# A vision tower on one core: the convolution's bias and the first layernorm's rows from one short line

## The chip, the cores and the metric

The kernel runs on one core of one Trainium2 chip. Times are device microseconds of that core. TensorE is called PE in the profile (PEld is its weight loads), VectorE is DVE, ScalarE is ACT, GpSimd is POOL, SyncE is SP. Before the change the median of three runs is 130.71 us (130.52 to 131.06).

## What is computed

Two images of 32 x 128 x 128 go through a patch embedding, a transformer of two layers with linear attention, one more linear attention and a mixed feed-forward layer. The change touches only the start of it:

```
patches = im.reshape(b, c, hp, P, wp, P)                     # 8 x 8 patches, 256 per image
x = einsum('bchpwq,dcpq->bhwd', patches, conv_w)             # contraction over 2048
x = x.reshape(b, hp * wp, -1) + conv_b                       # 256 tokens x 128
for i in range(2):
    y = _ln(x, ln1_g[i], ln1_b[i])                           # (x - mean) * rsqrt(var + eps) * g + b
    qkv = y @ qkv_w[i]
    ...                                                      # softmax of q and k, context, output, feed-forward
```

## The kernel before

The program of each engine is written out by hand, and each engine runs it in order; semaphores tie them together. Tokens lie on the 128 partitions, in two tiles for each image. SyncE issues all loads on one queue (L262 is the helper), in the order of L273 to L296: five pieces of embed_sb, which holds the convolution's weights and the first image's patches, with the bias tile convb_sb after the third; then the first half of the second image's patches, the broadcast load of norm_rows_sb[0] (gain and offset of the first layernorm, one row of 256 numbers written to all partitions), the key weights, small_sb (the identity for transposes, and columns), the query weights, and the rest.

TensorE multiplies in fp32; one product shows as two MATMUL records. It starts with products of ones (L311, warm_up), then adds the 16 chunks of image 0 into two banks (L320), each chunk as soon as its piece of embed_sb is there, and closes each bank with a bias product (L325): all ones, 128 x 128, times convb_sb, whose first row is the bias and whose other rows are zero. It goes on with chunks 0 to 5 of image 1, waits for the normalised y of image 0, turns it (L329), does chunks 6 and 7, and then the keys and queries of image 0 (L341, L347 for queries, L353, L360 for keys), each split in a high and a low part. L360 reads yT_lo, which VectorE makes. Chunks 8 to 15 and the bias of image 1 are worked in between; before the last bias product stand mix_fc_masks (L425 and L427, over nine rows). Then k and q of image 0 are turned (L366, L371), the keys of y are formed (L376) and y of image 1 is turned (L329 again).

The first layernorm of image 0 goes over four engines. VectorE takes the moments out of the bank (L929) and their aggregate (L935), ScalarE copies x out of it (L1514), VectorE centres and multiplies by the gain (L939), GpSimd raises the variance to the power of -0.5 for both tiles at once (L1782), VectorE scales and adds the offset (L944). ScalarE rounds the key and query weights and the turned y to their high parts (L1514), VectorE makes their low parts (L962).

The lines of VectorE around the load are:

```
dve.wait_ge(conv_done, 2)
moments(0, 1, CONV_BANK[0][1][:, 0:D]).then_inc(moments_done, 1)
dve.wait_ge(mean1_ready, 1)
dve.wait_ge(x_ready, 1)
dve.wait_ge(loaded["rg"], 16)
centre_and_gain(0, 0).then_inc(centred1, 1)
dve.wait_ge(moments_done, 2)
mean_and_variance(0, 1, stats).then_inc(mean1_ready, 1)
```

Of the kernel before, what the change touches and what calls it, by code (L numbers as in the profile page):

```python
# [12 lines left out]
P = 128  # L13
# [3 lines left out]
TILES = TOKENS // P  # L17
D = 128
KCONV = CHANNELS * PATCH * PATCH // P
# [34 lines left out]
CONV_AT = (0, 1, 4, 8, 12, KCONV)  # L54
CONV_PIECES = len(CONV_AT) - 1


def build(nc, small, convb, norm_rows0, norm_rows1, embed0, patches1, qkv_w, rest_w, rows, mix, fc_w, proj_w,
          head_w, aqkv_w, aout_w, out):
    with ExitStack() as ctx:  # L60
        def sb(name, shape, dt=F32):
            return ctx.enter_context(nc.sbuf_tensor(name, shape, dt))

        def sem(name):
            return ctx.enter_context(nc.semaphore(name))
# [14 lines left out]

        convb_sb = sb("convb_sb", [P, D])
        norm_rows_sb = [sb(f"norm_rows_sb{l}", [P, GROW]) for l in range(LAYERS)]
# [41 lines left out]
        def bias_row(name, n=0, width=D):  # L124
# [24 lines left out]
        kexp = sb("kexp", [P, PAIRS, TOKENS])  # L149
        ktok = sb("ktok", [P, TILES, INNER])  # L150
        q = sb("q", [P, TILES, INNER])
        qn = sb("qn", [P, TILES, INNER])
# [28 lines left out]
        bank = [ctx.enter_context(nc.psum_tensor(f"bank{i}", [P, 512], F32)) for i in range(8)]  # L181

        HROW_BANK = bank[6]
        CONV_BANK = [(bank[1], bank[5]), (bank[3], bank[6])]
# [29 lines left out]
        loaded = {n: sem(f"loaded_{n}") for n in (  # L214
            "aout", "aqkv", "cb", "embed0", "embed1", "embed2", "embed3", "embed4", "fc", "head",
            "mix", "patches1a", "patches1b", "proj", "qkv0k", "qkv0q", "qkv1", "rest0", "rest1",
            "rg", "rows", "small", "v0")}
        aqkv_weight_high, attention3_columns, attention3_ready, attention3_turned, attention_done, centred1 = (
# [33 lines left out]
        y_ready, y_turned = (  # L252
            sem(n) for n in ("y_ready", "y_turned",))
        consts_set = sem("consts_set")
        stored = sem("stored")
# [4 lines left out]
        def _(sp):  # L260
            def load(dst, src, name):
                sp.dma_start(dst, src).then_inc(loaded[name], 16)  # L262
# [12 lines left out]
            load_embed(4, 8, "embed2")  # L275
            load(convb_sb[:], convb, "cb")
            load_embed(8, 12, "embed3")
            load_embed(12, 16, "embed4")
            load_patches(0, 8, "patches1a")
            load(norm_rows_sb[0][:], norm_rows0.to_broadcast([P, GROW]), "rg")  # L280
            load(qkvw[0][:, INNER:2 * INNER], qkv_w[0][:, INNER:2 * INNER], "qkv0k")
# [25 lines left out]
        def _(pe):  # L307
# [15 lines left out]

            def conv_bias(i, t):
                return nc.tensor.matmul(CONV_BANK[i][t][:, 0:D], ones[:, 0:P], convb_sb[:], start=False, stop=True)  # L325

# [194 lines left out]
            conv(0, 6, 7)  # L521
            conv(0, 7, 8)
            pe.wait_ge(loaded["embed3"], 16)
            conv(0, 8, 9)
# [6 lines left out]
            conv(0, 14, 15)  # L531
            conv(0, 15, 16)
            pe.wait_ge(loaded["cb"], 16)
            conv_bias(0, 0).then_inc(conv_done, 1)
            conv_bias(0, 1).then_inc(conv_done, 1)
            pe.wait_ge(loaded["patches1a"], 16)
            conv(1, 0, 2)
            conv(1, 2, 4)
            conv(1, 4, 6)
# [25 lines left out]
            conv(1, 12, 14)  # L565
            conv(1, 14, 16)
            conv_bias(1, 0).then_inc(conv_done, 1)
            pe.wait_ge(k_exp_ready, 4)
            turn_k(0, 0, 1).then_inc(k_turned, 1)
            pe.wait_ge(coefficients_ready, 1)  # L570
            mix_fc_masks()
            conv_bias(1, 1).then_inc(conv_done, 1)
            pe.wait_ge(q_shifted, 2)
# [353 lines left out]
        def _(dve):  # L927
            def moments(i, t, src):
                return nc.vector.bn_stats(stats[i][:, t, 0:6], src)  # L929
# [4 lines left out]
            def mean_and_variance(i, t, of):  # L934
                return nc.vector.bn_aggr(mv[i][:, t, :], of[i][:, t, :])  # L935
# [159 lines left out]
            dve.wait_ge(conv_done, 2)  # L1095
            moments(0, 1, CONV_BANK[0][1][:, 0:D]).then_inc(moments_done, 1)
            dve.wait_ge(mean1_ready, 1)
            dve.wait_ge(x_ready, 1)
            dve.wait_ge(loaded["rg"], 16)
            centre_and_gain(0, 0).then_inc(centred1, 1)  # L1100
            dve.wait_ge(moments_done, 2)
            mean_and_variance(0, 1, stats).then_inc(mean1_ready, 1)
            dve.wait_ge(mean1_ready, 2)
            dve.wait_ge(x_ready, 2)
            centre_and_gain(0, 1).then_inc(centred1, 1)
            dve.wait_ge(deviation1_ready, 1)
            scale_and_offset(0, 0).then_inc(y_ready, 1)
            dve.wait_ge(centred1, 2)
# [403 lines left out]
        def _(act):  # L1512
            def evict(dst, src):
                return nc.scalar.activation(dst, src, ACT.Copy)  # L1514
# [49 lines left out]
            def gelu3(i, c):  # L1564
                src = FC3_BANK[i][c // 2][:, (c % 2) * TOKENS:(c % 2 + 1) * TOKENS]
                return nc.scalar.activation(hid3[i][:, c, :], src, ACT.Gelu_apprx_tanh, bias=fcb[:, c:c + 1])  # L1566

            act.wait_ge(moments_done, 1)
            evict(x[0][:, 0, :], CONV_BANK[0][0][:, 0:D]).then_inc(x_ready, 1)
# [403 lines left out]
```

## Time and profile before

| | |
|---|---|
| median of three runs | 130.71 us |
| the profiled execution | 130.16 us, of which 128.4 us are span |
| TensorE busy | 117.3 us, 91% of the span |
| VectorE, ScalarE, GpSimd busy | 75.5, 63.8, 48.7 us |
| chain that ended last | TensorE 60%, VectorE 14%, DMA 9% |
| data moved | 12.18 MB, nearly all in the first 33 us |

The span runs from the first to the last instruction of one execution; the median of the runs is 0.55 us above the profiled one. A row of a timeline gives the start, the time from there to the end of a merged group, the engine, the line and the operation, and in brackets how long the engine was idle before it and what it waited for. Records of pipelined products overlap, so the pace of TensorE is read from the starts, not from the durations.

### The profile page before, as it was taken

The numbers are of one execution on the slowest core, as the hardware profiler recorded it, in microseconds if no ns is written. First come the engines' busy times: TensorE is split into PE (matmuls) and PEld (weight loads), VectorE is DVE, ScalarE is ACT, GpSimd is POOL, SyncE is SP. The second block draws the span as 40 slices with busy tenths as digits, with TensorE's granted clock in tenths as the row PEclk, the third lists the DMA queues.
The fourth block names the chain that finished last, engine by engine and source line by source line (L and its number), as shares of the span: only waits on it lengthen the run. The fifth ranks groups of instructions, "written<-read, shape, count | busy, mean of one in ns | idle before, by whom it ended". The sixth has DMA issues, their size and how long they took to land.

```text
span 128.4 us, 2242 instructions
## 1 busy us (share of the span) xinstructions
PE 117.3 (91%) x852; PEld 101.4 (79%) x852; DVE 75.5 (59%) x236; ACT 63.8 (50%) x151; POOL 48.7 (38%) x60
## 2 busy tenths in 40 slices
PE   6999969999999999998999798769889988999991
PEld 6999968986976798996856687757588777998990
DVE  5000384988678963779999866348588477155002
ACT  3000153745578586477774459633872835423520
POOL 0000024043896584416759546096309022032000
PEclk9999999999999999999999999999999999999999
DMA  4999899999100000000000000000000000000101
GB/s 106 373 428 416 242 434 370 406 421 398 50 0 0 0 3 5 0 0 0 0 0 5 0 0 3 0 5 3 0 0 0 0 0 5 0 0 0 61 0 61
DMA packets 3884, 12.18 MB, mean 95 GB/s; under 512 B 441, under 2 KB 1817, under 8 KB 3618
## 3 DMA queue, kind: packets, MB, share of 16 engines
q1 hardware_dynamic: 3874, 12.05, 24.8%
q8 instruction: 6, 0.10, 0.3%
q14 instruction: 4, 0.03, 0.1%
HBM read 11.65 MB, written 0.39 MB: 94 GB/s over the span
## 4 chain that ended last, share of the span: by engine, by line
PE 60%; DVE 14%; DMA 9%; ACT 7%; POOL 4%; issue 3%; SPq 3%; DVEq 0%; POOLq 0%
DMA norm_rows_sb<-in_norm_rows 9%; PE bank L505 6%; PE bank L376 4%; PE bank L419 4%; PE bank L400 4%; PE bank L320 3%; SPq L262 3%; PE bank L341 3%; PE bank L371 3%; PE bank L393 2%; PE bank L353 2%; PE bank L491 2%; PE bank L329 2%; PE bank L407 2%; POOL rstd L1782 2%
## 5 line engine op out<-in xcount | busy, mean ns | idle before, releaser
L1782 POOL TENSOR_TENSOR rstd<-mv,minus_half 128x2 f32<-128x2 f32 x14 | 10.0, 714 | 39.4 <-DVE mv L935 39.1
L1800 POOL TENSOR_TENSOR qn<-q,rqsum 128x512 f32<-128x512 f32 x8 | 8.3, 1044 | 12.3 <-DVE rqsum L995 12.3
L1566 ACT ACTIVATE patches_sb<-bank,fcb 128x256 f32<-128x256 f32 x12 | 5.1, 471 | 10.5 <-PE bank L502 10.5
L1524 ACT ACTIVATE kexp<-bank,nkmax 128x256 f32<-128x256 f32 x16 | 7.5, 472 | 5.7 <-DVE nkmax L975 5.7
L419 PE MATMUL bank<-restw,hid 128*128 128x128 f32 x64 | 8.8, 281 | 1.0 <-ACT hid L1540 1.0
L505 PE MATMUL bank<-projw,patches_sb 128*128 128x192 f32 x48 | 9.4, 331 | 0.0
L400 PEld LDWEIGHTS bank<-cw,qT 128*128 128x128 f32 x64 | 7.8, 192 | 1.6 <-issue 1.0
L419 PEld LDWEIGHTS bank<-restw,hid 128*128 128x128 f32 x64 | 7.8, 191 | 1.6 <-ACT hid L1540 1.4
L400 PE MATMUL bank<-cw,qT 128*128 128x128 f32 x64 | 8.4, 277 | 0.4 <-DVE x L1010 0.4
L320 PEld LDWEIGHTS bank<-embed_sb 128*128 128x128 f32 x64 | 8.1, 203 | 0.1
L320 PE MATMUL bank<-embed_sb 128*128 128x128 f32 x64 | 8.2, 285 | 0.0
L1540 ACT ACTIVATE hid<-bank,small_sb 128x256 f32<-128x256 f32 x16 | 6.5, 473 | 3.2 <-PE bank L414 3.2
L505 PEld LDWEIGHTS bank<-projw,patches_sb 128*128 128x128 f32 x48 | 7.6, 189 | 0.5 <-ACT patches_sb L1566 0.4
L376 PE MATMUL bank<-ktok,y 128*128 128x512 f32 x16 | 8.0, 612 | 0.0
L1514 ACT ACTIVATE x<-bank 128x128 f32<-128x128 f32 x4 | 1.1, 282 | 13.8 <-DVE stats L929 13.8
L1536 ACT ACTIVATE cw<-bank,rksum 128x128 f32<-128x128 f32 x16 | 4.8, 366 | 6.4 <-PE bank L393 5.3
L320 PE MATMUL bank<-embed_sb,patches_sb 128*128 128x128 f32 x64 | 7.9, 277 | 0.0
L929 DVE BATCH_NORM_STATS2 stats<-bank 128x6 f32<-128x128 f32 x4 | 1.1, 275 | 11.0 <-PE bank L325 11.0
L320 PEld LDWEIGHTS bank<-embed_sb,patches_sb 128*128 128x128 f32 x64 | 7.5, 192 | 0.1
L975 DVE TENSOR_REDUCE nkmax<-bank 128x2 f32<-128x512 f32 x8 | 5.4, 688 | 3.0 <-PE bank L360 2.9
L1792 POOL TENSOR_TENSOR xb<-x,rows_sb 128x256 f32<-128x256 f32 x8 | 5.9, 737 | 1.9 <-DVE y L944 1.2
L311 PE MATMUL bank<-ones 128*128 128x192 f32 x16 | 5.2, 487 | 1.1 <-DVE stats L1083 1.1
(167 smaller groups left out, 335.5 us busy)
## 6 DMA issues: line engine op xcount, KB each, us to landing
embed_sb<-in_embed SPq DMA_DIRECT2D x3, 768.0 KB, 6.9
patches_sb<-in_patches SPq DMA_DIRECT2D x2, 1024.0 KB, 11.9
restw<-in_rest_w SPq DMA_DIRECT2D x2, 768.0 KB, 16.5
qkvw<-in_qkv_w SPq DMA_DIRECT2D x3, 256.0 KB, 11.1
qkvw<-in_qkv_w SPq DMA_DIRECT2D x1, 768.0 KB, 16.6
fcw<-in_fc_w SPq DMA_DIRECT2D x1, 768.0 KB, 19.1
embed_sb<-in_embed SPq DMA_DIRECT2D x1, 576.0 KB, 4.3
aqkvw<-in_aqkv_w SPq DMA_DIRECT2D x1, 576.0 KB, 11.8
```

The lines of the kernel that those rows point to most:

```text
L311: mm = nc.tensor.matmul(dst[:, 0:E], ones[:, 0:P], ones[:], start=True, stop=True)
L320: mm = nc.tensor.matmul(CONV_BANK[i][t][:, 0:D], left, embed_sb[:, c, 0:D], start=(c == 0), stop=False)
L376: return nc.tensor.matmul(YK_BANK[s][:], y[s % IMAGES][:, t, :], ktok[:, t, :], start=(t == 0), stop=(t == TILES - 1))
L400: mm = nc.tensor.matmul(ATT_BANK[s][t][:, 0:D], qT[:, t, c * P:(c + 1) * P], cw[:, c, :], start=(c == 0), stop=(c == PAIRS - 1))
L419: mm = nc.tensor.matmul(FF2_BANK[s][t][:, 0:D], hid[:, c, t * P:(t + 1) * P], ff2w(s // IMAGES, c), start=(c == 0), stop=(c == FC - 1))
L505: return nc.tensor.matmul(PROJ3_BANK[i][t][:, 0:E], hid3[i][:, c, t * P:(t + 1) * P], projw[:, c, :], start=(c == 0), stop=(c == HC - 1))
L975: return nc.vector.tensor_reduce(nkmax[i][:, 2 * b:2 * b + 2], K_BANK[s][b][:].rearrange("p (c t) -> p c t", c=2), AX_X, ALU.max, negate=True)
L1524: return nc.scalar.activation(kexp[:, c, :], K_BANK[s][c // 2][:, (c % 2) * TOKENS:(c % 2 + 1) * TOKENS], ACT.Exp, bias=nkmax[i][:, c:c + ...
L1540: return nc.scalar.activation(hid[:, c, :], FF1_BANK[s][c // 2][:, (c % 2) * TOKENS:(c % 2 + 1) * TOKENS], ACT.Gelu, bias=col("ff1_b", s / ...
L1782: return nc.gpsimd.tensor_tensor(rstd[i][:], mv[i][:, :, 1], minus_half[:], ALU.pow)
L1792: return nc.gpsimd.tensor_tensor(xb[i][:], x[i][:], row.unsqueeze(1).to_broadcast([P, TILES, D]), ALU.add)
L1800: return nc.gpsimd.tensor_tensor(qn[:, t, :].rearrange("p (h d) -> p h d", h=HEADS), q[:, t, :].rearrange("p (h d) -> p h d", h=HEADS), rq ...
```

## The change

The bias tile and the broadcast load go. One line of 384 numbers (bias, gain, offset) is loaded on one partition, in a corner of ktok, which isn't written before. Products over one row (ones[0:1] times the line) spread it: the bias straight into the convolution's banks, in the middle of the accumulation, for image 0 after chunk 7 and for image 1 after its chunk 1; gain and offset into a free bank, from which ScalarE copies them to norm_rows_sb[0] before its first other work. The last chunk closes each bank now. In VectorE's program the aggregate of the second tile moves ahead of the first centring, the wait for the load becomes one for the copied rows, and the first scaling waits for the first centring.

```diff
@@ build
-        convb_sb = sb("convb_sb", [P, D])
+        first_row_sb = ktok[0:1, 0, 0:D + GROW]
+        FIRST_ROWS_BANK = bank[2]
@@ SyncE
-            load(convb_sb[:], convb, "cb")
+            load(first_row_sb, first_row, "first_row")
             load_embed(8, 12, "embed3")
             load_embed(12, 16, "embed4")
             load_patches(0, 8, "patches1a")
-            load(norm_rows_sb[0][:], norm_rows0.to_broadcast([P, GROW]), "rg")
@@ TensorE
-            def conv_bias(i, t):
-                return nc.tensor.matmul(CONV_BANK[i][t][:, 0:D], ones[:, 0:P], convb_sb[:], start=False, stop=True)
+            def conv_last(i, t):
+                c = KCONV - 1
+                left = (embed_sb[:, c, D + t * P:D + (t + 1) * P] if i == 0
+                        else patches1_sb[:, c, t * P:(t + 1) * P])
+                return nc.tensor.matmul(CONV_BANK[i][t][:, 0:D], left, embed_sb[:, c, 0:D], start=False, stop=True)
+
+            def conv_bias(i):
+                for t in range(TILES):
+                    mm = nc.tensor.matmul(CONV_BANK[i][t][:, 0:D], ones[0:1, 0:P], first_row_sb[:, 0:D],
+                                          start=False, stop=False)
+                return mm
+
+            def first_norm_rows():
+                return nc.tensor.matmul(FIRST_ROWS_BANK[:, 0:GROW], ones[0:1, 0:P], first_row_sb[:, D:D + GROW],
+                                        start=True, stop=True)
             conv(0, 7, 8)
+            pe.wait_ge(loaded["first_row"], 16)
+            conv_bias(0)
+            first_norm_rows().then_inc(first_rows_done, 1)
             pe.wait_ge(loaded["embed3"], 16)
...
-            conv(0, 15, 16)
-            pe.wait_ge(loaded["cb"], 16)
-            conv_bias(0, 0).then_inc(conv_done, 1)
-            conv_bias(0, 1).then_inc(conv_done, 1)
+            conv_last(0, 0).then_inc(conv_done, 1)
+            conv_last(0, 1).then_inc(conv_done, 1)
             pe.wait_ge(loaded["patches1a"], 16)
             conv(1, 0, 2)
+            conv_bias(1)
             conv(1, 2, 4)
...
-            conv(1, 14, 16)
-            conv_bias(1, 0).then_inc(conv_done, 1)
+            conv(1, 14, 15)
+            conv_last(1, 0).then_inc(conv_done, 1)
             pe.wait_ge(k_exp_ready, 4)
             turn_k(0, 0, 1).then_inc(k_turned, 1)
             pe.wait_ge(coefficients_ready, 1)
             mix_fc_masks()
-            conv_bias(1, 1).then_inc(conv_done, 1)
+            conv_last(1, 1).then_inc(conv_done, 1)
@@ VectorE
             moments(0, 1, CONV_BANK[0][1][:, 0:D]).then_inc(moments_done, 1)
+            dve.wait_ge(moments_done, 2)
+            mean_and_variance(0, 1, stats).then_inc(mean1_ready, 1)
             dve.wait_ge(mean1_ready, 1)
             dve.wait_ge(x_ready, 1)
-            dve.wait_ge(loaded["rg"], 16)
+            dve.wait_ge(first_rows_ready, 1)
             centre_and_gain(0, 0).then_inc(centred1, 1)
-            dve.wait_ge(moments_done, 2)
-            mean_and_variance(0, 1, stats).then_inc(mean1_ready, 1)
             dve.wait_ge(mean1_ready, 2)
             dve.wait_ge(x_ready, 2)
             centre_and_gain(0, 1).then_inc(centred1, 1)
             dve.wait_ge(deviation1_ready, 1)
+            dve.wait_ge(centred1, 1)
             scale_and_offset(0, 0).then_inc(y_ready, 1)
@@ ScalarE
+            act.wait_ge(first_rows_done, 1)
+            evict(norm_rows_sb[0][:], FIRST_ROWS_BANK[:, 0:GROW]).then_inc(first_rows_ready, 1)
             act.wait_ge(moments_done, 1)
```

## Rows read from the trace of the kernel before

**Rows 1.** The page, busy time: us, share of the span, instructions.
```profile
PE 117.3 (91%) x852; PEld 101.4 (79%) x852; DVE 75.5 (59%) x236; ACT 63.8 (50%) x151; POOL 48.7 (38%) x60
```

**Rows 2.** The chain that ended last, in order of time: start, us, what.
```profile
4.39 11.18 DMA norm_rows_sb<-in_norm_rows
```

**Rows 3.** Timeline of TensorE's products, 8 to 20 us.
```profile
8.03 5.52 PE L320 MATMUL bank<-embed_sb 128*128 128x128 f32 x48
13.39 0.61 PE L325 MATMUL bank<-convb_sb,ones 128*128 128x128 f32 x4
13.88 2.94 PE L320 MATMUL bank<-embed_sb,patches_sb 128*128 128x128 f32 x24
17.82 0.44 PE L329 MATMUL bank<-small_sb,y 128*128 128x128 f32 x2 [0.99 <-DVE y L944]
18.09 1.06 PE L320 MATMUL bank<-embed_sb,patches_sb 128*128 128x128 f32 x8
...
19.11 0.28 PE L353 MATMUL bank<-yT_hi,qkw_lo 128*128 128x256 f32 x1
19.36 0.39 PE L360 MATMUL bank<-yT_lo,qkw_hi 128*128 128x256 f32 x1
19.58 0.39 PE L341 MATMUL bank<-qkw_hi,yT_hi 128*128 128x512 f32 x1
```

**Rows 4.** Timeline of the first image's layernorm on VectorE and GpSimd.
```profile
13.81 0.30 DVE L929 BATCH_NORM_STATS2 stats<-bank 128x6 f32<-128x128 f32 x1 [10.96 <-PE bank L325]
15.70 0.35 DVE L939 SCALAR_TENSOR_TENSOR xg<-x,mv,norm_rows_sb 128x128 f32<-128x128 f32 x1 [1.12 <-DMA norm_rows_sb<-in_norm_rows]
16.31 0.81 POOL L1782 TENSOR_TENSOR rstd<-mv,minus_half 128x2 f32<-128x2 f32 x1 [15.87 <-DVE mv L935]
17.15 0.61 DVE L944 SCALAR_TENSOR_TENSOR y<-xg,rstd,norm_rows_sb 128x128 f32<-128x128 f32 x2 [0.60 <-POOL rstd L1782]
```

**Rows 5.** Stretches by busy times, clock, DMA share, GB/s; then an issue.
```profile
12.40:12.80 0.40, 0.40 (x6) 0.40 (x5) 0.00 (x0) 0.00 (x0) 0.00 (x0) 1.00 1.00 420
13.20:13.60 0.40, 0.40 (x6) 0.40 (x5) 0.00 (x0) 0.00 (x0) 0.00 (x0) 1.00 0.44 67
...
convb_sb<-in_convb SPq DMA_DIRECT2D x1, 64.0 KB, 5.5
```

**Rows 6.** Timeline, the high and low part of the turned y.
```profile
18.29 0.39 ACT L1514 ACTIVATE yT_hi<-bank 128x256 fp32r<-128x256 f32 x1 [0.39 <-PE bank L329]
18.89 0.42 DVE L962 TENSOR_TENSOR yT_lo<-bank,yT_hi 128x256 fp32r<-128x256 f32 x1
```

**Rows 7.** Timeline of TensorE around the nine-row products, and that stretch's busy times.
```profile
26.04 0.38 PE L366 MATMUL bank<-small_sb,kexp 128*128 128x128 f32 x2
26.35 0.61 PE L425 MATMUL bank<-mix_sb,alpha_mask_e 9*128 9x16 f32 x4
26.79 0.30 PEld L427 LDWEIGHTS bank<-mix_sb,alpha 9*128 9x128 f32 x2
26.82 0.57 PE L427 MATMUL bank<-mix_sb,alpha 9*128 9x192 f32 x2
27.31 0.49 PE L325 MATMUL bank<-convb_sb,ones 128*128 128x128 f32 x2
27.64 0.60 PE L366 MATMUL bank<-small_sb,kexp 128*128 128x128 f32 x4
...
26.30:27.30 1.00, 1.00 (x8) 0.74 (x6) 0.99 (x4) 0.59 (x2) 0.71 (x1) 1.00 1.00 412
```

**Rows 8.** Timeline up to the turn of the second image's y.
```profile
26.59 1.04 POOL L1800 TENSOR_TENSOR qn<-q,rqsum 128x512 f32<-128x512 f32 x1 [5.43 <-DVE rqsum L995]
28.50 0.70 POOL L1782 TENSOR_TENSOR rstd<-mv,minus_half 128x2 f32<-128x2 f32 x1 [0.87 <-DVE mv L935]
28.51 1.88 PE L376 MATMUL bank<-ktok,y 128*128 128x512 f32 x4
29.39 0.35 DVE L939 SCALAR_TENSOR_TENSOR xg<-x,mv,norm_rows_sb 128x128 f32<-128x128 f32 x1 [0.96 <-ACT x L1514]
29.65 0.61 DVE L944 SCALAR_TENSOR_TENSOR y<-xg,rstd,norm_rows_sb 128x128 f32<-128x128 f32 x2
30.32 0.44 PE L329 MATMUL bank<-small_sb,y 128*128 128x128 f32 x2
```

More of the change, by code:

```diff
@@ L54, with build @@
 CONV_AT = (0, 1, 4, 8, 12, KCONV)
-CONV_PIECES = len(CONV_AT) - 1
-def build(nc, small, convb, norm_rows0, norm_rows1, embed0, patches1, qkv_w, rest_w, rows, mix, fc_w, proj_w,
+def build(nc, small, first_row, norm_rows1, embed0, patches1, qkv_w, rest_w, rows, mix, fc_w, proj_w,
           head_w, aqkv_w, aout_w, out):
@@ L214, in build @@
         loaded = {n: sem(f"loaded_{n}") for n in (
-            "aout", "aqkv", "cb", "embed0", "embed1", "embed2", "embed3", "embed4", "fc", "head",
+            "aout", "aqkv", "embed0", "embed1", "embed2", "embed3", "embed4", "fc", "first_row", "head",
             "mix", "patches1a", "patches1b", "proj", "qkv0k", "qkv0q", "qkv1", "rest0", "rest1",
-            "rg", "rows", "small", "v0")}
+            "rows", "small", "v0")}
         aqkv_weight_high, attention3_columns, attention3_ready, attention3_turned, attention_done, centred1 = (
@@ L253, in build @@
             sem(n) for n in ("y_ready", "y_turned",))
+        first_rows_done, first_rows_ready = sem("first_rows_done"), sem("first_rows_ready")
         consts_set = sem("consts_set")
@@ L1943 @@
     norm_rows = [np.concatenate([a[T + "ln1_g"][l], a[T + "ln1_b"][l]])[None] for l in range(LAYERS)]
-    convb = np.zeros((P, D), np.float32)
-    convb[0] = a[T + "conv_b"]
+    first_row = np.concatenate([a[T + "conv_b"][None], norm_rows[0]], axis=1)
     rows = np.concatenate([a[T + "out_b"].reshape(-1), a[T + "ff2_b"].reshape(-1), a[T + "head_b"],
@@ L1957 @@
     host = {
-        "small": small, "convb": convb, "norm_rows0": norm_rows[0], "norm_rows1": norm_rows[1], "embed0": embed0, "patches1": patches1,
+        "small": small, "first_row": first_row, "norm_rows1": norm_rows[1], "embed0": embed0, "patches1": patches1,
         "qkv_w": np.stack(qkv), "rest_w": np.stack(rest), "rows": rows,
```

## The prediction

> **What bounds the kernel now.** I read the page first: TensorE is busy for most of the span [rows 1], so what counts is when it has nothing to do. Then the chain that ended last, in order of time: its longest early piece is the broadcast load of the first layernorm's rows, issued at 4.39 us and landed at 15.57 [rows 2]. Then the timelines. TensorE runs 12 chunks of the first image's convolution from 8.03 to 13.39 without a gap, 48 records in 5.36 us, so a record of 128 columns takes 0.112 us (a product is two records, 0.22 us). The bias products follow, then 24 records for the second image, over at 13.88 + 24 x 0.112 + 0.10 = 16.67 (the 0.10 is the restart after a pause, priced below). The next product, the turn of y, starts at 17.82 [rows 3]. TensorE stands still for 1.15 us. The cause is VectorE: it waits 1.12 us for the rows, centres, takes the second tile's mean, GpSimd takes the root, VectorE scales, and only then can TensorE turn [rows 4].
>
> The first 30 us are one pipeline of four in-order engines. I follow two gates in it: the first image's keys and queries (record L341 at 19.58) and the turn of the second image's y at 30.32 [rows 3, 8]. The second image's work starts at the second gate, and the queues behind it shift with it, so I take the shift there to reach the end.
>
> **The loads.** The 64 KB tile and the 128 KB broadcast go; one line of 1.5 KB comes, in the tile's place of SyncE's queue. The tile landed 5.5 us after its issue at 2.11, at 7.6 [rows 5]. TensorE now waits for the short line ahead of chunk 8, with the other eight chunks queued behind; it gets there at 8.03 + 16 x 0.112 = 9.8 us. That is 2.2 us of slack, so the wait costs nothing; a line over 2.2 us later than the tile would stop TensorE. The broadcast seems dear beyond its bytes: from 420 GB/s the rate falls to 67 at 13.20, when its packets must be under way [rows 5]. Some three stretches of 0.4 us nearly empty are over 1 us, beside 192 KB at 410 GB/s, 0.47 us. I expect the loads behind it 1 to 1.8 us sooner. It will turn out that nothing needs them sooner.
>
> **TensorE before the first y.** Added:
> - the rows product: 256 columns, twice the width of a 0.112 us record, two records: 0.44 us;
> - the bias of image 0: four records, moved forward only: 0;
> - the bias of image 1: four records, brought here from behind the first y: 0.45 us;
> - going from products over 128 rows to products over one row and back, twice. The trace has no one-row product. The nearest are nine-row ones. Between the two records before them (26.04) and their start (26.35) lie 0.31 us where two records take 0.22: 0.09. The 16-column records hide a restart that 128 columns would show. Behind them, the full-height pair at 27.31 takes 0.33 instead of 0.22, 0.11 for the restart; and the 192-column pair lasts 0.49, where two streams of 0.16 (192/128 of 0.112) and 0.08 of the first weight load account for 0.40, so leaving costs 0.09 too [rows 7]. A change is thus 0.09 + 0.10 = 0.19, four are 0.76 us. From below they could be free; from above there is the second rival.
>
> Sum 0.44 + 0.45 + 0.76 = 1.65. Off it goes a pause of today: the second image's patches landed just when TensorE came to them, and the bias products and what follows stretch by 0.15 in all between 13.39 and the steady pace [rows 3]. TensorE is free for the turn at 16.67 + 1.65 - 0.15 = 18.17.
>
> **The first y.** The convolution ends 0.44 + 0.38 later, so VectorE's moments go from 13.81 to 14.63. Moments and means of both tiles now run ahead of the centring, which frees GpSimd sooner: 14.63 + about 1.1 = 15.7, root 0.81 to 16.6, two scalings 0.61 to 17.3 [rows 4]. VectorE's new wait for the copied rows and for its own centring is long over by then: ScalarE copies the rows around 10.6 us in 0.39, the price of its 128x256 copy at 18.29 [rows 6], and what is queued behind that copy (the eviction of x) isn't due before 14 us. Cost nothing. So y is ready 0.9 us before TensorE is: the wait for a load has become TensorE's own added work.
>
> The turn thus starts 0.35 later than now. Its successors catch up, since pauses fall away: today one of 0.05 ahead of the turn's second record, and one at L360, 0.25 after its forerunner at 19.11 where 0.115 is natural, with 0.22 instead of 0.115 behind it [rows 3]: 0.29 together. 0.35 - 0.29 = 0.06. yT_hi (0.39) and yT_lo (0.42) [rows 6] run from 18.57 and end at 19.44, and the product that reads yT_lo would come at 19.51: just in time. First gate: +0.1 us, 19.7. With today's loads (key weights split from 16.23 on), that work too would be over by 18.7, which is why the faster queue brings nothing.
>
> **Between the gates.** Here TensorE has four records fewer: 0.45 us, so it runs at -0.35 from 26 us on. VectorE has nothing less and runs at +0.1; GpSimd's root goes from 28.50 to 28.6 and ends at 29.3. The scaling of the second y starts at 29.65 today; its centring is held by a ScalarE copy that waits for TensorE's turned k, so it moves by -0.35, to 29.3, as the root allows, and y is ready at 29.9. TensorE: q normalised by GpSimd is there at 26.59 + 1.04 + 0.1 = 27.73, which takes back 0.1; the keys of y start at 28.51 - 0.25, four records of 0.43, and the turn comes at 30.0 to 30.1 instead of 30.32, and without the pause of 0.05 inside it [rows 8]. Second gate: -0.3 us.
>
> The median is 130.71; the profiled execution took 130.16, of which 128.4 is span. 130.71 - 0.3 = 130.4 (129.9 on the side of the profiled one).
>
> **The rivals.** *Changing the height of products is free.* For it: the four nine-row records at 26.35 keep a pitch of 0.117; against it, the gaps on both sides of them [rows 7]. TensorE would be free at 17.4, with y ready at 16.9; first gate -0.5, second gate -0.9, there held by VectorE and TensorE alike: 129.8.
>
> *One-row products don't overlap their weight loads.* Each of the 4 + 2 + 4 records would cost its load, 0.11, more: 1.1 us. It decides from the point where TensorE comes to the turn after about 18.2, when the pauses are used up. Turn at 19.2, first gate +1.15; VectorE's chain carries all of it, the root ends at 30.4, y at 31.0, second gate at 31.05: +0.7, 131.4. Against it: both weight loads of the 192-column pair lie within 0.30 us, from 26.79 on, while the first product ran from 26.82 [rows 7]. For it: 0.11 + 0.16 for the first record and 0.22 for the rest would also fit the 0.49.
> The Trainium skill (TensorE: Matmul & The Clock Gate, Part 3, The mechanism) says that a weight load overlaps products in flight only where the row groups differ; that is this rival. The full-height records of this trace share all rows and keep 0.112 us with their loads under them, so the trace speaks against the rule as it stands.
>
> *The queue gets no faster, or the short line is late.* The dip may belong to the moment and not to the broadcast. By the above today's landings are early enough: still 130.4. For a loss the line must land after 9.8 us, and to cost 0.5% after about 10.5; nothing in the queue speaks for it.
>
> *TensorE's clock falls* around the short products. It stays full through the nine-row stretch [rows 7]. At half speed a stretch of 2.5 us costs 1.2: 131.6.
>
> **How the numbers follow.** The forecast is 130.4, with 130.1 to 130.8 as its own range: 0.55, and 0.07 for the useless queue at the same time. Free changes: 0.17, and 0.02 for other gains. No overlap: 0.14. Clock or late line: 0.05. About 0.5% (0.65 us) is what a measurement of this kernel can tell from no change. Faster by more: 0.19 and the lowest tail of the forecast, 0.21; slower: 0.14 and most of the 0.05, 0.17 to the nearest; same 0.62. Without the clock case and the outer tails the range is 129.7 to 131.3.
>
> **What would show it.** Right: no DMA ahead of VectorE's centring; TensorE without idle time from 8 to 19 us; pauses or stretched pitches of 0.2 us at each end of a one-row group; the turn at 18.1 to 18.3 with y ready near 17.3; weights landed over 1 us sooner, and unused until then; near 400 GB/s at 13 us; the second turn at 30.0. Wrong: the turn at 17.5 (free changes) or past 18.6 (no overlap, a pitch over 0.2 in the one-row records); idle time ahead of L360 for yT_lo; a gain at the second gate that the end doesn't show.

## The result and the profile after

The changed kernel takes 130.09 us in the median of nine runs (129.66 to 130.53) where the kernel before, timed beside it, takes 130.87 (130.52 to 131.07): a ratio of 0.9941, with a 95% interval of 0.9922 to 0.9959, so 0.5 to 1.0 us less. The forecast was 130.4, a gain of 0.3: the sign was right, and the gain was more than twice as large.

Its profiled execution took 130.53 us, the slowest of the nine, with a span of 128.7. The one of before took 130.16, below all nine. So the two profiles side by side show a loss of 0.4 us, and the medians a gain of 0.8; most of what follows is about that difference.

TensorE's products in the profile after, from 8.7 us on (start, us, what); to be read beside [rows 3]:

```profile
8.70 1.95 PE L320 MATMUL bank<-embed_sb 128*128 128x128 f32 x16
10.57 0.71 PE L332 MATMUL bank<-ktok,ones 1*128 1x128 f32 x4
11.12 0.59 PE L337 MATMUL bank<-ktok,ones 1*128 1x256 f32 x2
11.64 3.39 PE L320 MATMUL bank<-embed_sb 128*128 128x128 f32 x28
14.87 0.61 PE L328 MATMUL bank<-embed_sb 128*128 128x128 f32 x4
15.32 1.06 PE L320 MATMUL bank<-embed_sb,patches_sb 128*128 128x128 f32 x8
16.31 0.71 PE L332 MATMUL bank<-ktok,ones 1*128 1x128 f32 x4
16.94 2.05 PE L320 MATMUL bank<-embed_sb,patches_sb 128*128 128x128 f32 x16
18.83 0.38 PE L342 MATMUL bank<-small_sb,y 128*128 128x128 f32 x2
...
20.37 0.39 PE L354 MATMUL bank<-qkw_hi,yT_hi 128*128 128x512 f32 x1
...
30.68 0.41 PE L342 MATMUL bank<-small_sb,y 128*128 128x128 f32 x2
```

No bracket stands behind a row: TensorE has no idle time up to the turn. The price of a change of height can be read off. 16 records from 8.70 end at 10.49, the one-row product starts at 10.57; its four records take 0.55 instead of 0.45; the 256-column pair takes 0.52 instead of 0.43; and 28 full-height records take 3.23 instead of 3.13. That is 0.08 + 0.10 going in and 0.09 + 0.10 going out, the 0.19 of the sum. The second group: 0.63 from 16.31 to 16.94 for 0.45 of records, and the 0.10 behind it.

The rest of the early path, on the other engines; compare [rows 4]:

```profile
11.75 0.38 ACT L1530 ACTIVATE norm_rows_sb<-bank 128x256 f32<-128x256 f32 x1 [9.74 <-PE bank L337]
15.30 0.30 DVE L944 BATCH_NORM_STATS2 stats<-bank 128x6 f32<-128x128 f32 x1 [12.45 <-PE bank L328]
16.23 0.61 DVE L954 SCALAR_TENSOR_TENSOR xg<-x,mv,norm_rows_sb 128x128 f32<-128x128 f32 x2
16.45 0.71 POOL L1800 TENSOR_TENSOR rstd<-mv,minus_half 128x2 f32<-128x2 f32 x1 [16.02 <-DVE mv L950]
17.20 0.62 DVE L959 SCALAR_TENSOR_TENSOR y<-xg,rstd,norm_rows_sb 128x128 f32<-128x128 f32 x2 [0.35 <-POOL rstd L1800]
```

The rows are copied in 0.38 us on an idle ScalarE, the centring waits for nothing, y ends at 17.8, and TensorE takes it up 1.0 us later.

The loads. The rate of a stretch of 0.4 us that was 67 GB/s at 13.20 [rows 5] is now (same columns, the last is GB/s):

```profile
13.20:13.60 0.40, 0.40 (x6) 0.40 (x5) 0.00 (x0) 0.00 (x0) 0.00 (x0) 1.00 1.03 378
```

and the second piece of embed_sb, behind whose products all others stand in TensorE's program, landed later than in the profile before. Issued at 1.17 in both, it took, after and then before:

```profile
embed_sb<-in_embed SPq DMA_DIRECT2D x1, 576.0 KB, 5.4
```
```profile
embed_sb<-in_embed SPq DMA_DIRECT2D x1, 576.0 KB, 4.3
```

That is why everything in the after profile starts 0.67 us later, at 8.70 instead of 8.03. The trace tells when each of a load's 16 parts landed: here 15 had landed by 5.07 us and the last came at 6.56. For the third piece it was 7.20 and 8.44. One straggling part is late, not the whole load. Taken from this start, the turn should come by the forecast at 18.17 + 0.67 = 18.84 and did at 18.83; the first gate at 19.68 + 0.67 = 20.35, measured 20.37; the second at 30.05 + 0.67 = 30.72, measured 30.68. The span, 128.74 against 128.37, is 0.37 longer, and the second gate 0.36 later: from there to the end both profiles take 98.06 us.

### The profile page after: what moved, and what is told of

Same layout as the page of the kernel before. It is cut to its first block, busy times and chain, and to the rows that moved or that the text cites. A ratio compares the mean times of both kernels' runs of the same rounds, so it can differ in the third digit from the quotient of the medians.

```text
span 128.7 us, 2247 instructions
## 1 busy us (share of the span) xinstructions
PE 117.3 (91%) x854; PEld 100.7 (78%) x854; DVE 75.4 (59%) x236; ACT 63.8 (50%) x152; POOL 48.5 (38%) x60
## 4 chain that ended last, share of the span: by engine, by line
PE 69%; DVE 13%; ACT 7%; DMA 4%; POOL 3%; issue 2%; SPq 0%
PE bank L320 11%; PE bank L518 6%; PE bank L389 4%; DMA embed_sb<-in_embed 4%; PE bank L432 4%; PE bank L413 4%; PE bank L384 3%; PE bank L354 3%; PE bank L406 2%; PE bank L366 2%; PE bank L504 2%; PE bank L420 2%; PE bank L342 2%; PE bank L398 2%; POOL qn L1818 2%
## 5 line engine op out<-in xcount | busy, mean ns | idle before, releaser
L320 PEld LDWEIGHTS bank<-embed_sb 128*128 128x128 f32 x60 | 7.2, 194 | 2.2 <-DMA embed_sb<-in_embed 1.9
L427 PE MATMUL bank<-yT_lo,ff1w_hi 128*128 128x256 f32 x16 | 5.1, 319 | 0.9 <-POOL yT_lo L1803 0.9
L1803 POOL TENSOR_TENSOR yT_lo<-yT,yT_hi 128x256 fp32r<-128x256 f32 x4 | 2.9, 730 | 7.8 <-ACT yT L1533 7.8
```

Of the source, the lines that this page charges most:

```text
L320: mm = nc.tensor.matmul(CONV_BANK[i][t][:, 0:D], left, embed_sb[:, c, 0:D], start=(c == 0), stop=False)
L427: return nc.tensor.matmul(FF1_BANK[s][c // 2][:, (c % 2) * TOKENS:(c % 2 + 1) * TOKENS], ff1w_parts[l][0][:, c * P:(c + 1) * P], yT_lo[i][ ...
```

## The experiments

One table for all. "Start" is TensorE's first record after the third piece of embed_sb, "turn" the first turn of y, "gate 1" the first query product, "gate 2" the turn of the second image's y, "patches" the landing of the second half of the second image's patches; us in the profiled execution. With the patches split in two, "patches" is the first of the two pieces; the second landed at 22.1, 22.8 and 20.8 us in the three kernels, and none waited for it. The last two columns are from the timed runs beside the kernel before.

| kernel | start | turn | gate 1 | patches | gate 2 | span | median (before) | ratio, 95% interval |
|---|---|---|---|---|---|---|---|---|
| before | 8.03 | 17.82 | 19.58 | 21.5 | 30.32 | 128.4 | 130.87 | |
| after | 8.70 | 18.83 | 20.37 | 20.8 | 30.68 | 128.7 | 130.09 (130.87) | 0.994, 0.992 to 0.996 |
| after, again | | | | | | | 129.83 (130.84) | 0.992, 0.989 to 0.996 |
| before, second profile | 8.43 | 17.67 | 19.43 | 21.4 | 30.18 | 128.2 | one run, 130.09 | |
| before, third profile | 7.57 | 17.64 | 19.40 | 22.5 | 30.91 | 129.0 | one run, 131.09 | |
| full height | 8.24 | 17.72 | 19.26 | 20.6 | 29.59 | 127.6 | 129.36 (130.84) | 0.990, 0.987 to 0.994 |
| order only | 7.64 | 16.84 | 18.94 | 22.6 | 31.05 | 129.1 | 130.81 (130.84) | 1.000, 0.997 to 1.002 |
| rows only | 8.15 | 17.56 | 19.18 | 21.5 | 29.93 | 127.9 | 129.76 (130.91) | 0.992, 0.989 to 0.995 |
| before, 352 KB ahead | 7.56 | 18.72 | 20.48 | 23.6 | 32.06 | 130.1 | 131.79 (130.91) | 1.005, 1.003 to 1.008 |
| after, 352 KB ahead | 8.67 | 19.00 | 20.54 | 22.0 | 30.86 | 128.9 | 130.38 (130.91) | 0.997, 0.994 to 1.000 |
| bias only | 8.55 | 18.25 | 19.82 | 22.9 | 30.96 | 128.9 | 130.15 (130.91) | 0.995, 0.992 to 0.997 |
| before, patches split | 8.42 | 18.38 | 20.14 | 19.4 | 30.91 | 129.0 | 130.45 (131.05) | 0.995, 0.993 to 0.998 |
| order, patches split | 8.29 | 17.39 | 19.61 | 19.2 | 30.37 | 128.4 | 130.24 (131.05) | 0.994, 0.992 to 0.997 |
| full height, split | 8.43 | 17.79 | 19.33 | 17.8 | 30.03 | 128.0 | 129.29 (131.05) | 0.987, 0.985 to 0.990 |

In every row the span minus gate 2 is 97.9 to 98.1 us. So what happens up to 30 us reaches the end one to one, and the second gate is all that has to be explained.

Two more distances hold in the profiles. With the kernel before's order of VectorE the turn comes 2.25 or 2.26 us after the rows have landed, in all five profiles of such kernels. And gate 2 comes a fixed time after TensorE begins chunk 8 of the second image: 8.3 us where the bias products stand at the end, 7.9 where they don't, with 0.1 for the restart where TensorE had to wait for the patches; only the last kernel below falls out of this. So the rows set gate 2 only as long as the patches are there when TensorE comes to chunk 8.

### The two kernels once more

The kernel before, unchanged:

> The kernel before, unchanged, for a second profiled execution. In the profile on which the prediction rests, TensorE was ready for its second piece of loads (5.98 us) later than they landed (5.5), and the layernorm's rows landed at 15.57. The changed kernel's own profile has the second piece landing at 6.6 us because one DMA engine lags by 1.1 us. Theory A (loads land later in most executions than in that first profile, and the kernel before passes all of such a delay on, because its chain runs through the landing of the rows): here the span minus 128.4 equals the landing of the rows minus 15.57, within 0.15 us. Theory B (landings have nothing to do with the difference between executions): the rows land at 15.5 to 15.6 whatever the time is.

It took 130.09 us; the rows landed at 15.41 and TensorE started 0.40 us later than in the first profile of it, yet the turn came 0.15 sooner. Its early path follows the landing of the rows and hides a late start: theory A is right on that much, and the span is 0.2 shorter where the rows landed 0.16 sooner. But at 130.1 us this is again an early execution, so it doesn't show what makes the usual one slower.

The changed kernel, unchanged:

> The changed kernel, unchanged. Theory A: the turn of the first y starts 10.13 us after the first record of the chunk that follows the third piece (8.70 to 18.83 in its first profile), whatever the start is, so a profile with a start at 8.0 has a turn at 18.2 and a span of 128.0 to 128.1. Theory B: the span doesn't follow the start. Median 0.6 to 0.9 us below the kernel before, as measured already.

Timed again it is at 129.83 us against 130.84, ratio 0.9923 (0.9891 to 0.9956). Its profiled execution took 226 us: TensorE ran at half its pace (16 records in 3.87 us instead of 1.79, with a granted clock of 1.00 in the profile's rows), for a reason that nothing here shows. It says nothing on the gates, though its patches landed at 19.3, sooner than in any profile of the kernel before. So whether the changed kernel's span follows its start was not seen on a second profile of the same kernel. Its closest relative, the run with 352 KB ahead, starts at 8.67 and turns 10.33 us later (10.13 in the after profile); it had waited before its start, which costs 0.10 for the restart, and waited 0.1 for the first half of the patches on the way.

### Full-height products

```diff
-        first_row_sb = ktok[0:1, 0, 0:D + GROW]
+        first_row_sb = ktok[:, 0, 0:D + GROW]
-            load(first_row_sb, first_row, "first_row")
+            sp.wait_ge(line_zeroed, 1)
+            load(first_row_sb[0:1, :], first_row, "first_row")
-  ... ones[0:1, 0:P], first_row_sb ...
+  ... ones[:, 0:P], first_row_sb ...
+            nc.vector.memset(first_row_sb, 0.0).then_inc(line_zeroed, 1)
```

> The changed kernel with the line loaded into row 0 of a zeroed 128-row tile and spread by products over all 128 rows, so that products never change their height. If the changes of height cost 0.19 us each, four of them, all on TensorE's path ahead of the first y: TensorE is free for the turn 0.75 us sooner than in the changed kernel, the first gate comes 0.7 sooner, the second 0.7, and the median lies 0.7 us below the changed kernel's, 1.4 to 1.5 below the kernel before's. If changes of height are free or hidden: as the changed kernel. Pitches of 0.112 with no gap at either end of the group.

Measured: 129.36 us, 1.48 below the kernel before; the changed kernel is 0.78 and 1.01 below it in its two comparisons, so by the medians this one is 0.5 to 0.7 better. By the clock alone that isn't settled: its interval (0.9869 to 0.9936) and that of the changed kernel timed with it (0.9891 to 0.9956) overlap. The trace settles it. TensorE in this kernel:

```profile
10.12 0.61 PE L334 MATMUL bank<-ktok,ones 128*128 128x128 f32 x4
10.57 0.60 PE L339 MATMUL bank<-ktok,ones 128*128 128x256 f32 x2
11.01 3.29 PE L322 MATMUL bank<-embed_sb 128*128 128x128 f32 x28
14.13 0.61 PE L330 MATMUL bank<-embed_sb 128*128 128x128 f32 x4
14.58 1.07 PE L322 MATMUL bank<-embed_sb,patches_sb 128*128 128x128 f32 x8
15.48 0.61 PE L334 MATMUL bank<-ktok,ones 128*128 128x128 f32 x4
15.93 1.95 PE L322 MATMUL bank<-embed_sb,patches_sb 128*128 128x128 f32 x16
17.72 0.38 PE L344 MATMUL bank<-small_sb,y 128*128 128x128 f32 x2
```

0.45, 0.44, 3.12: no gap at either end. From start to turn it takes 9.48 us; the changed kernel takes 10.13. 0.10 of the 9.48 is a restart after a short wait at its start (1.88 for 16 records instead of 1.79). So four changes of height cost 0.75 on the path, against 0.76 by the sum, and from the start to gate 2 this kernel takes 0.63 us less (21.35 against 21.98), with its restart in it. The rival by which changes are free is out; so is the one by which one-row products don't overlap their weight loads, since their records keep 0.112 us between the ends. The rule of the Trainium skill quoted with the forecast (TensorE: Matmul & The Clock Gate, Part 3, The mechanism) doesn't hold for this kernel's products, one-row or full-height. But at a change of height something like it shows. The weight loads at the first product of a group, in the full-height kernel and then twice in the profile after:

```profile
10.02 0.53 PEld L334 LDWEIGHTS bank<-ktok,ones 128*128 128x128 f32 x4
```
```profile
10.57 0.52 PEld L332 LDWEIGHTS bank<-ktok,ones 1*128 1x128 f32 x4
11.64 0.52 PEld L320 LDWEIGHTS bank<-embed_sb 128*128 128x128 f32 x4 [0.33 <-issue]
```

At full height the load starts 0.10 us before its product (10.12). Where the height changes, it starts with it, at 10.57 and 11.64. So the 0.10 behind each change looks like one load that isn't hidden; that reading was not tested further.

### Only VectorE's order

```diff
+            dve.wait_ge(moments_done, 2)
+            mean_and_variance(0, 1, stats).then_inc(mean1_ready, 1)
             dve.wait_ge(mean1_ready, 1)
             dve.wait_ge(x_ready, 1)
             dve.wait_ge(loaded["rg"], 16)
             centre_and_gain(0, 0).then_inc(centred1, 1)
-            dve.wait_ge(moments_done, 2)
-            mean_and_variance(0, 1, stats).then_inc(mean1_ready, 1)
...
             dve.wait_ge(deviation1_ready, 1)
+            dve.wait_ge(centred1, 1)
             scale_and_offset(0, 0).then_inc(y_ready, 1)
```

> The kernel before, with both loads and all products as they were; only VectorE's program takes the second tile's mean ahead of the wait for the rows, as the changed kernel does. By the accounting the root then runs from 14.9 us while the rows are still on their way, y is ready 0.85 us sooner, the turn at 16.95; but ScalarE's rounding of the query weights waits for their landing at 17.25, so yT_hi comes 0.36 us sooner at most, and the median falls by 0.35 us: as much as the changed kernel was forecast to gain. Rival: the changed kernel's gain comes from the loads and not from the order, then this one gains 0.1 us or less.

The kernel is as fast as the one before (1.000, 0.997 to 1.002). Yet the turn came at 16.84, 0.98 sooner (0.87 expected), and the first gate 0.64 sooner, where 0.36 was to be the most; the query weights, which were to set it, landed at 16.96 instead of 17.25. Then:

```profile
21.26 0.28 PE L360 MATMUL bank<-yT_lo,qkw_hi 128*128 128x256 f32 x1
22.66 2.05 PE L320 MATMUL bank<-embed_sb,patches_sb 128*128 128x128 f32 x16 [1.11 <-DMA patches_sb<-in_patches]
```

TensorE stands before chunk 8 of the second image until 22.66: the second half of its patches has just landed. All that was gained is given back to a load that the prediction had dismissed. In the profile before it landed at 21.5, 0.5 us ahead of TensorE (21.48 and 22.02). This is where theory C comes from: that load is a second gate of its own.

### One part of the line alone

Rows by the line, bias as before (64 KB tile, full-height products at the end), against the changed kernel:

```diff
+            load(convb_sb[:], convb, "cb")
             load(first_row_sb, first_row, "first_row")
...
-            conv_bias(0)
             first_norm_rows().then_inc(first_rows_done, 1)
...
-            conv_last(0, 0).then_inc(conv_done, 1)
-            conv_last(0, 1).then_inc(conv_done, 1)
+            conv(0, 15, 16)
+            pe.wait_ge(loaded["cb"], 16)
+            conv_bias_tile(0, 0).then_inc(conv_done, 1)
+            conv_bias_tile(0, 1).then_inc(conv_done, 1)
...
-            conv_bias(1)
...
-            conv(1, 14, 15)
-            conv_last(1, 0).then_inc(conv_done, 1)
+            conv(1, 14, 16)
+            conv_bias_tile(1, 0).then_inc(conv_done, 1)
```

> The changed kernel with the bias as it was before (64 KB tile, full-height products at the ends); only gain and offset come from the line, by one one-row product. TensorE has 0.44 + 0.38 us more ahead of the first y than the kernel before, y is ready at 17.3, the turn at 17.4; VectorE's low parts of the weights end at 18.6, so the keys wait for yT_lo and the first gate comes 0.3 us sooner than before, the second 0.3 sooner. Theory A adds 0.4 us for late loads: 0.6 to 0.8 below the kernel before, as the changed kernel. If moving the bias is what brings the gain, this one gains 0.3 less than the changed kernel.

129.76 us, 1.15 below the kernel before, at least as good as the changed kernel. Its path from gate 1 to gate 2 takes 10.75 us, as before (10.74), where the changed kernel takes 10.31: moving the bias does pay 0.43 there. Ahead of the turn it costs more than that: from start to turn this kernel takes 9.41 us, of which 0.10 is the restart after a wait, and the changed one 10.13, so 0.82 for four records (0.44) and two changes of height (0.38). By these numbers the one-row bias loses 0.4 us in sum, and the gain is all in the rows and in what goes with them; the medians point the same way, within their noise. The expected 0.6 to 0.8 was exceeded. The patches landed at 21.50 here, 0.14 ahead of TensorE, though the broadcast is gone: 14 of their 16 parts were there by 19.8, and the last was late.

Bias by the line, rows by the broadcast as before, VectorE's new order; against the changed kernel:

```diff
             load_patches(0, 8, "patches1a")
+            load(norm_rows_sb[0][:], norm_rows0.to_broadcast([P, GROW]), "rg")
...
-            first_norm_rows().then_inc(first_rows_done, 1)
...
-            dve.wait_ge(first_rows_ready, 1)
+            dve.wait_ge(loaded["rg"], 16)
...
-            act.wait_ge(first_rows_done, 1)
-            evict(norm_rows_sb[0][:], FIRST_ROWS_BANK[:, 0:GROW]).then_inc(first_rows_ready, 1)
```

> The changed kernel with gain and offset loaded by the broadcast as before; only the bias comes from the line, by one-row products, and VectorE's new order stays. TensorE has 0.45 + 0.76 - 0.15 us more ahead of the first y than the kernel before and is free for the turn at 17.7; the rows land at 15.4 and y is ready at 16.9. First gate 0.4 us sooner than in the kernel before, then four records fewer: second gate 0.75 sooner. So 0.4 us better than the changed kernel in its forecast, if the rows product's 0.44 us is what that costs; late loads shift all of it. Rival (the landing of the rows is the dear part): it isn't better than the kernel before by more than 0.3 us. In the trace the rate of the loads falls again under 100 GB/s where the broadcast runs, if the dip belongs to the broadcast.

130.15 us, 0.76 below the kernel before. It was not 0.4 better than the changed kernel but at best equal to it. The patches landed at 22.9 and TensorE waited for them:

```profile
PEld bank L322 <- DMA patches_sb<-in_patches: 0.7, 1, 0.7
DVE xg L955 <- DMA norm_rows_sb<-in_norm_rows: 0.5, 1, 0.5
```

(waits: us in total, times, longest). What the expectation left out is again that load. The dip is there as well, but shallower than expected: 128 GB/s from 13.2 to 13.6, not under 100.

### 352 KB more ahead

The value and head weights are loaded right after the first half of the patches instead of later, in either kernel:

```diff
             load_patches(0, 8, "patches1a")
+            load(qkvw[0][:, 2 * INNER:], qkv_w[0][:, 2 * INNER:], "v0")
+            load(headw[:], head_w, "head")
...
-            load(headw[:], head_w, "head")
...
-            load(qkvw[0][:, 2 * INNER:], qkv_w[0][:, 2 * INNER:], "v0")
```

> The kernel before with the value weights and the head's weights (352 KB, 0.86 us at 410 GB/s) loaded right after the first half of the patches, ahead of the layernorm's rows. Theory A: the rows land 0.86 us later and all of it goes through: +0.8 to +0.9 us in the median. Theory B (the wait for the rows is covered by something else): under +0.3.

> The changed kernel with the same 352 KB loaded right after the first half of the patches. Theory A: nothing on its path waits for a load behind that place; key weights land at 15.3 to 15.5 instead of 14.5 and are rounded in time: as the changed kernel within 0.15 us, so 0.6 to 0.9 below the kernel before, and 1.5 below the kernel before with the same delay. Rival (the sooner loads are a real part of the gain): it loses 0.5 us or more.

The kernel before loses 0.9 us (131.79 against 130.91, interval 0.4 to 1.0), and its turn is 0.9 later: as expected. But the number doesn't prove the path. The edit delays the patches as well; they landed at 23.62, and TensorE, done with the keys and queries, waited 0.70 us for them. In this profile the patches set gate 2 and not the rows, so that 0.9 came out is partly luck. Its dip moved with the broadcast. Stretches of 0.4 us in this kernel:

```profile
13.20:13.60 0.40, 0.40 (x6) 0.40 (x5) 0.00 (x0) 0.00 (x0) 0.00 (x0) 1.00 0.98 366
...
14.40:14.80 0.40, 0.40 (x7) 0.40 (x5) 0.07 (x1) 0.28 (x1) 0.00 (x0) 1.00 0.22 56
14.80:15.20 0.40, 0.40 (x6) 0.40 (x5) 0.00 (x0) 0.00 (x0) 0.00 (x0) 1.00 0.37 82
```

366 GB/s where 67 was, 56 where the broadcast now is: the slow stretch belongs to the broadcast of one row of 1 KB to 128 partitions. The changed kernel is at 130.38, 0.53 below the kernel before, where it was 0.78 and 1.01 below in the two comparisons without this; so it loses 0.25 to 0.5. That is more than theory A's 0.15 and at the edge of the rival's 0.5, and suggests that sooner loads are a real part of the gain; the intervals of the comparisons overlap, so it doesn't show it. In its profile the patches landed at 22.0, 1.0 ahead of TensorE, so no wait for them was seen there.

### A third look at the kernel before

> The kernel before, unchanged, a third profiled execution. Theory C: what holds the kernel before in most of its executions isn't the landing of the rows alone but that of the second half of the second image's patches, on its slowest DMA engine; it lands at 21.4 to 21.5 in the two profiles of about 130.1 us, 0.5 before TensorE comes to it, and later in the executions of 130.8 us. So if this execution takes 130.6 or more, TensorE waits for these patches near 22 us, for as long as the time is above 130.1; if it takes 130.1, it doesn't wait. Theory D (the span follows only from how late TensorE starts on the convolution): the wait isn't there and the start is later by the difference.

This one took 131.09 us, a usual execution. TensorE:

```profile
21.75 0.28 PE L360 MATMUL bank<-yT_lo,qkw_hi 128*128 128x256 f32 x1
22.51 2.05 PE L320 MATMUL bank<-embed_sb,patches_sb 128*128 128x128 f32 x16 [0.48 <-DMA patches_sb<-in_patches]
```

0.76 us from record to record instead of 0.12: a wait of 0.64 for patches that landed at 22.46, while start, turn and gate 1 are no later than in the two early executions. Gate 2 is 0.73 later than in the second profile, the span 0.8. Theory C as expected, theory D out. The same load was issued at 7.50 and 7.55 in the two and took, second profile and then third:

```profile
patches_sb<-in_patches SPq DMA_DIRECT2D x1, 1024.0 KB, 13.9
```
```profile
patches_sb<-in_patches SPq DMA_DIRECT2D x1, 1024.0 KB, 14.9
```

Nearly all of the load came no later than before: 15 of its 16 parts had landed by 21.12 in the second profile and by 21.34 in the third. The last part followed at 21.38 in the one and at 22.46 in the other. In the run with the new order alone it was 21.19 and 22.61.

### The patches in two pieces

```diff
+            load_patches(8, 12, "patches1b")
             load(aqkvw[:], aqkv_w, "aqkv")
-            load_patches(8, 16, "patches1b")
+            load_patches(12, 16, "patches1c")
...
+            pe.wait_ge(loaded["patches1c"], 16)
             conv(1, 12, 14)
```

> The kernel before with the second half of the patches loaded in two pieces: chunks 8 to 11 ahead of the 576 KB attention weights (1.4 us sooner, about 20.1 us), chunks 12 to 15 behind them, at 21.5 as before, where TensorE needs them at 24. Nothing else changes. Theory C: its usual execution is now like the early ones of the kernel before, 130.1: 0.5 to 0.8 us below it in the median. If the patches aren't waited for in the usual execution: within 0.2 us of the kernel before.

130.45 us against 131.05 (0.9954, 0.9933 to 0.9975): 0.6 us (0.3 to 0.9) by this edit alone, with everything else as in the kernel before. Its profiled execution is no early one, and now the rows show: they landed at 16.13, 0.56 later than in the first profile, and the turn is 0.56 later. TensorE comes to chunk 8 without a wait, 3.2 us after the patches.

> The kernel before with VectorE's new order and the patches in two pieces; rows and bias are loaded and multiplied as before. In the run with the new order alone the turn came 0.9 us sooner and all of it was lost to a wait of 1.3 us for the patches. Theory C: with the patches sooner the order is worth 0.3 to 0.6 us on top of the split: 0.9 to 1.3 below the kernel before, so as good as the changed kernel or better. If the order brings nothing even so: as the split alone.

130.24, 0.81 below. Only 0.2 more than the split alone, within the intervals of the two, so what the order brings on top isn't settled; 0.9 to 1.3 was too much. It has the changed kernel's speed with no one-row product in it.

> The changed kernel with full-height products and the patches in two pieces, the version that should beat all others. In the full-height run the patches landed 1.0 us before TensorE came to them, so by theory C the split adds little: 1.4 to 1.7 us below the kernel before, at most 0.2 below the full-height version. If late patches still cost it in its usual executions, 0.3 or more below it.

129.29 us, ratio 0.9873 (0.9846 to 0.9900): the lowest median of all kernels here, 1.8 us below the kernel before. Against the full-height version without the split (0.9903, 0.9869 to 0.9936) no difference can be claimed, as expected: there the patches already come 1.1 us early (20.59 and 21.73). In its profile gate 2 is 10.70 after gate 1 instead of 10.33, since VectorE waits for the small masks (mix_sb), which landed at 24.09; the chain to gate 2 runs from there over the normalised q (GpSimd, 26.73) and its turn (27.82), which in the full-height kernel stands at 27.38. The load stands behind the patches in the queue:

```profile
DVE alpha L1036 <- DMA mix_sb<-in_mix: 0.3, 1, 0.3
```

## Why the prediction was right, and where its size was off

*What bounds the kernel.* Right for the profile that it read, where the turn follows the landing of the rows and gate 2 follows the turn. Wrong for the usual execution, where the patches come later still and set gate 2: with VectorE's new order alone the turn came 1 us sooner, and the time stayed the same.

*TensorE's added work, 1.65 us.* Right in every term: 0.43 for the rows, 0.44 between the gates for the bias, 0.18 to 0.19 for each change of height, read off the after profile and confirmed by the full-height kernel.

*The short line* cost nothing. *ScalarE's copy* cost nothing. *The first y* was ready 1.0 us before TensorE (0.9 forecast).

*The gates*: with the start that its profile had, turn, gate 1 and gate 2 were hit within 0.04 us, and the steps between as well: y of the second image was expected to be ready at 29.9 + 0.67 and was at 30.59, with its root done at 29.83.

*The loads.* Right: the dip is the broadcast's, and it cost about what was said. From the landing of the first half of the patches to that of the second half it was 7.64 us and is 6.04, so 1.6 us less. By the clock they came only 0.7 sooner, and the key weights 0.8, because this profile's loads were 0.9 to 1.1 late before that. Wrong: "nothing needs them sooner". That step looked at the key and query weights and passed over the patches, whose landing lay 0.5 us ahead of TensorE in the one profile at hand and lies behind it in others: the third profile shows 0.64 us of wait, and loading them sooner in the kernel before is worth 0.6 us. The broadcast's removal does just that: in the changed kernel they landed at 20.8, 2.0 ahead of TensorE, even with a late start. So 0.3 us were forecast and 0.8 measured. The missing 0.5 is this wait, priced at nothing: about 0.6 to 0.7 by the third profile and the split, less some 0.2 for the changed kernel's usual start, later than 8.03 (an estimate: its median lies 0.44 below its profile, which started 0.67 late).

*The time beside the profile.* The prediction saw that the profiled 130.16 lay 0.55 below the median and took the gap as a constant. For the larger part it was this wait; the rest, by the split kernel's profile, is the landing of the rows, which scatters too. A check by the gates: the median before, 130.87, is 0.7 above the profiled one, so gate 2 is usually near 31.0, as in the third profile (30.91). The profile was an uncommon one: of the 86 timed runs of the kernel before, 4 took 130.3 us or less.

*The call.* By its own measure, 0.65 us for what can be told from no change, the gain of 0.78 is a "faster by more", to which it gave 0.21, and not the "same" with its 0.62. The median of 130.09 also lies just under the range of 130.1 to 130.8 that it gave its own case, and it missed by no more than 0.3 because its base, 130.71, was 0.16 below the later median of the kernel before; in the gain the miss is 0.5. So the accounting of TensorE and of the gates was right, and not by luck, while the size of the gain was not foreseen, since one wait was left out.

*What is open*: why one part of a load straggles, how often the patches are late, and how often the start is. The start may belong to the change. The third piece of embed_sb landed at 7.4 to 7.6 us in all five profiles of kernels with the old loads in the old order or with 352 KB moved ahead, and at 8.1 to 8.6 in the six profiles at full pace of kernels with the short line. But it landed at 8.2 in the two kernels before with split patches, and at 7.1 in the profile of 226 us of the changed kernel, so no run tells what moves it. The changed kernel has given up 1.15 us of idle time that hid a late start, so by its accounting a start at 8.4 costs it 0.4 that the kernel before doesn't pay (that one turned at 17.67 from such a start). That fits its scatter of 129.7 to 130.5, but is argued from single profiles.

## What to carry to other kernels

A load that lands 0.5 us before it is needed isn't free in a program whose landings scatter by a microsecond: list every wait with its slack, not only those that show idle time, and compare the profiled time with the median before trusting a cover. When a broadcast is replaced by products, count what the switch between products of different height costs at each end; zeroed rows and full-height products avoid it. And when a gain at an early point of a path is shown by the trace but not by the clock, look for the next load in line.

## What the runs showed of the hardware

- Changing between products over 128 rows and over one row costs 0.18 to 0.19 us each time (profile after; 0.75 for four against the full-height kernel); one-row records of 128 columns otherwise keep 0.112 us, like full-height ones.
- Around the first broadcast of a 1 KB row to 128 partitions the rate in stretches of 0.4 us fell to 49 to 61 GB/s at its lowest in five profiles and to 77 to 128 in the three others that have it (both split kernels, bias only), where the loads around it ran at 360 to 470. Moved in the queue (352 KB ahead), the dip moved with it; without the broadcast it was gone.
- The landing of the same 1 MB load, issued within 0.05 us, scattered by 1.1 us between two executions of the same kernel (21.38 and 22.46), nearly all of it in the last of its 16 parts.
